# Counting the second sort's blocks on ScalarE, half of them ahead of the first projection loop

## The chip, the cores and the metric

The kernel runs on one core of a Trainium2 chip. The metric is the device time of one execution in microseconds (us). Five engines with their own instruction queues share the work: TensorE (PE in the profile, its weight loads PEld), VectorE (DVE), ScalarE (ACT), GpSimd (POOL), and SyncE (SP), which here only starts transfers. They meet only at semaphores. Before and after were timed in the same manner; three runs of the kernel before are shown here.

## The reference

Two layers of a graph network over 3125 nodes with 256 features and 50,000 edges. Each layer adds a sum over edges, an attention over all nodes, and a mixture of experts. What matters here is the first layer's part over edges and its attention:

```python
xn = _layernorm(x, axis=-1)
x = x + _L0_gnn_ref(xn, edge_index, edge_weight, ...) + _L0_mix_ref(xn[None], ...)[0]

# in _L0_mix_ref
qkv = x @ W_qkv + b_qkv
q, k, v = jnp.split(qkv, 3, axis=2)
q = q - jnp.mean(q, axis=2, keepdims=True)
k = k - jnp.mean(k, axis=2, keepdims=True)
q2 = q * q
k2 = k * k
q2s = jnp.sum(q2, axis=2, keepdims=True)
k2s = jnp.sum(k2, axis=2, keepdims=True)
k2 = _l2_normalize(k2 / (k2s + EPS_DIV), axis=-2)
q2 = _l2_normalize(q2 / (q2s + EPS_DIV), axis=-1)
kv = jnp.einsum('bnc,bnd->bcd', k2, v)
t2 = jnp.einsum('bnc,bcd->bnd', q2, kv) / math.sqrt(N)
attn = v + t2
return attn @ W_out + b_out
```

Layer 0 sums its edges by source node (`segment_sum(vals, src)`), layer 1 by destination node (`segment_sum(msg, dst)`). The kernel therefore sorts the edges twice, once by each.

## The kernel before

The program is a chain of stages with a barrier between them. The change lies in the first, `stage_project0`, which does three things side by side.

**Two counting sorts of the edges.** The 50,000 edges lie as 128 x 391 numbers. The first sort puts them into 25 bins by source, the second into 98 blocks of 32 nodes by destination (100 are counted, 4 in each of 25 turns). A sort has these steps: the bin of each edge (`split_index`); the count of each bin in each partition (`rank_count_bins`: DVE compares all 391 bins with one number and adds up the hits with the same instruction, line 114); sums over partitions by two matmuls on PE (`ps_rank`); the starts of the bins (`rank_bases`); and for each bin the slot of every edge in it (`rank_slots_bins`: compare, running sum, predicated copy, lines 139, 142 and 145). From the slot comes the row to which an edge's record is written.

**The first sort's scatter on POOL.** `scatter_records` issues one indirect DMA for each of the 391 columns (line 245). It waits for `s_rows` twice: at column 0, for the rows of the first 48 columns, which DVE makes first (`SLOT_GROUPS`), and at column 48, for those of the remaining 343. The stage ends when all scatters have landed, and the next stage reads the sorted list.

**The first projection and the attention.** After the sort's rows DVE makes the statistics of x (lines 199 to 214), signals `s_var`, waits until ACT has taken the root (`s_std`), and makes a few products of weights. Then 25 turns over tiles of 125 nodes, spread over three engines:

- PE transposes the normed tile, adds the tile before last to `ps_kv` and `ps_cn` (`add_kv`), and, once ACT has copied the transposed tile to SBUF (`keep_xT`, signal `s_xTs`), multiplies by the weights (line 781).
- DVE adds the biases (from line 675), norms a tile two ahead (line 669), counts four of the second sort's blocks (line 114), turns ACT's sums into negative means (line 687), and scales k2 (lines 690 to 694).
- ACT copies xT of the next tile (line 497), copies q and k with their sums (507), waits for the negative means, squares q and k (510, 511), squares again (514), and waits for k2 and squares it (516). Each accumulating instruction is followed in the profile by a read of the accumulator.

Behind the loop PE closes its sums (lines 805, 806), waits for `s_cnt`, and makes the second sort's sums over partitions (809, 810). A second loop of 25 turns follows, called the slot loop here: PE and ACT make the attention's output, DVE adds it to x (lines 744 to 748) and makes the slots of four blocks (`rank_slots_bins`). `Order` numbers an engine's own steps so that it can wait for its own results: `settle` waits for all of them, `settle_alone` does so with a separate instruction.

Of the kernel before, what the change touches and what calls it, by code (L numbers as in the profile page):

```python
# [12 lines left out]
BF16 = mybir.dt.bfloat16  # L13
# [4 lines left out]
P = 128  # L18
# [3 lines left out]
TN = 25  # L22
# [148 lines left out]
def split_index(o, whole, rest, key, size):  # L171

    o.done(o.eng.tensor_scalar(whole, key, -(size - 1) / 2.0, 1.0 / size, ALU.add, ALU.mult))
    o.settle()
    o.done(o.eng.tensor_scalar(whole, whole, MAGIC, MAGIC, ALU.add, ALU.subtract))
    o.settle()
    o.done(o.eng.scalar_tensor_tensor(rest, whole, -float(size), key, ALU.mult, ALU.add))
    o.settle()
# [110 lines left out]
def stage_project0(nc, a, k):  # L289
# [5 lines left out]
    with ExitStack() as ctx:  # L295
# [30 lines left out]
        first = m.sb("first", [P, P])  # L326
        pad = m.sb("pad", [P, 4 * G0_TILES])
# [61 lines left out]
        s_rows = m.sem("rows_known")  # L389
        s_scat = [m.sem(f"scattered{i}") for i in range(2)]  # L390
# [100 lines left out]
        def _(act):  # L491
            o = Order(act, s_a)
            act.wait_ge(s_var, 1)
# [5 lines left out]
            def step(t, last):  # L499
                if not last:  # L500
                    keep_xT(t + 1)
                o.enter(t, 3) if not last else None
# [13 lines left out]
                nc.scalar.activation(k4[:], k2[:], ACT.Square).then_inc(s_k4, 1)  # L516
                o.leave(TN - 1) if not last else None
# [6 lines left out]
            act.sem_inc(s_sq, 1)  # L524
            act.wait_ge(s_kvd, 1)
# [25 lines left out]
        def _(dve):  # L551
# [62 lines left out]

            for n, g in enumerate(SLOT_GROUPS):
# [9 lines left out]
                nc.vector.tensor_copy(row0[:, g], running[:, 0, g]).then_inc(s_rows, 1)  # L625
            group_bins(o, k["bin0"][:], column, reached, ps_vf, ps_qk, iota_g, G0_BINS, G0_N + 8, s_col, s_row, 0)

            o.done(nc.vector.tensor_copy(key[:], dst[:]))
            o.done(nc.vector.memset(k["record1"][:], 0.0))  # L630
            o.done(nc.vector.memset(cnt[:], 0.0))
            o.settle()
            split_index(o, rest[:], whole[:], key[:], G1_BINS)
            o.done(nc.vector.scalar_tensor_tensor(bin_of1[:], rest[:], -NOWHERE, whole[:], ALU.mult, ALU.max))
            o.done(nc.vector.tensor_scalar(slot[:, ELAST:], k["iota"][:, 0:EC - ELAST], float(P), float(P * G1_N + P - 1), ALU.mult, ALU.add))
            o.done(nc.vector.tensor_copy(k["record1"][:, :, 0], src[:]))
            o.done(nc.vector.tensor_copy(k["record1"][:, :, 1], rest[:]))
# [34 lines left out]
            def step(t, norm_ahead):  # L672
                o.enter(t, 3 + R1) if not isinstance(t, int) else None
# [11 lines left out]
                rank_count_bins(o, bin_of1[:], cnt, mask, k["iota"], t * R1, R1)  # L685
# [19 lines left out]
            o.settle()  # L705
            dve.sem_inc(s_cnt, 1)
# [2218 lines left out]
```

## Time and profile before

| | us |
|---|---|
| three runs: lowest, median, highest | 2844.44, 2845.75, 2851.44 |
| profiled execution, its time | 2843.54 |
| its span, first to last instruction | 2841.8 |
| DVE busy in the span | 1835.1 (65%) |
| POOL busy | 1814.0 (64%) |
| PE busy | 1659.2 (58%) |
| ACT busy | 850.7 (30%) |
| line 245, this stage's scatters | 391 issues, 414.0 busy, 159.7 idle ahead of them |

The engines' shares are means over the whole span. The first stage fills the first 580 us of it, and what counts for it is read there: which engine's last instruction the next stage waits for. The time of the profiled execution is 1.7 us above its span, which is what lies around the first and the last instruction.

### The profile page before, as it was taken

Reading aid. Unit: us, or ns where it says so; the run is one execution under the profiler, and the core shown is the slowest. Engines: PE = TensorE matmul, PEld = TensorE weight load, DVE = VectorE, ACT = ScalarE, POOL = GpSimd, SP = SyncE. Lnnn points to the kernel's source line nnn. Section 1 sums busy time; section 2 is a strip of 40 time slices with the busy share of each in tenths; the row PEclk is TensorE's granted clock in tenths of the full one; section 3 lists DMA queues with packets and bytes.
Section 4 is the critical chain, followed back from the end, with each engine's and each line's share of the span. In section 5 each row is a group of like instructions: output and inputs, shape, how many; then the busy total and the mean of one; then the engine's idle time right before and its main releaser. Section 6 shows DMA issues by size and latency. Waiting matters only on the chain. (4 is left out here: it accounts for less than half of the span.)

```text
span 2841.8 us, 52033 instructions
## 1 busy us (share of the span) xinstructions
PE 1659.2 (58%) x12361; PEld 1202.8 (42%) x12362; DVE 1835.1 (65%) x5560; ACT 850.7 (30%) x2657; POOL 1814.0 (64%) x1828
## 2 busy tenths in 40 slices
PE   0488444236666666424999657655666655401997
PEld 0254333124444454312666434344555544301665
DVE  8776699568777777621222256488888888865322
ACT  0144111024444444101333234323333333301231
POOL 3777777757777777777777777377777777600000
PEclk9999666568888888657999878767666676655998
DMA  7000000053333333042333330233333337321000
GB/s 225 9 22 20 2 2 1 1 197 105 107 107 107 107 106 106 21 168 89 86 87 86 100 90 21 46 106 106 105 106 106 106 106 150 82 69 58 10 18 18
DMA packets 169775, 224.90 MB, mean 79 GB/s; under 512 B 77731, under 2 KB 129226, under 8 KB 169513
## 3 DMA queue, kind: packets, MB, share of 16 engines
q0 software_dynamic: 74368, 138.96, 18.3%
q1 hardware_dynamic: 95270, 84.55, 10.4%
q14 instruction: 105, 0.86, 0.1%
q8 instruction: 32, 0.52, 0.1%
HBM read 184.08 MB, written 39.29 MB: 79 GB/s over the span
## 5 line engine op out<-in xcount | busy, mean ns | idle before, releaser
L2112 POOL DMA_INDIRECT e_rows<-mid_table,rec x488 | 486.1, 996 | 184.1 <-issue 137.7
L245 POOL DMA_INDIRECT mid_sorted<-p_record,p_row x391 | 414.0, 1059 | 159.7 <-issue 122.2
L922 POOL DMA_INDIRECT e_rows<-mid_table,e_rec x440 | 420.0, 954 | 150.4 <-issue 91.4
L245 POOL DMA_INDIRECT mid_sorted<-keep_record,keep_row x391 | 393.7, 1007 | 129.4 <-issue 121.1
L1084 PE MATMUL e_ps_A<-e_rows,e_hot 128*125 128x260 f32 x880 | 306.5, 481 | 0.0
L2374 ACT ACTIVATE room<-room 128x66 f32 x488 | 126.1, 258 | 260.7 <-ACT room L2374 209.8
L1084 PEld LDWEIGHTS e_ps_A<-e_rows,e_hot 128*125 128x125 f32 x880 | 188.0, 237 | 25.1
L1069 PE MATMUL e_ps_T<-e_identb,e_hot 128*125 128x128 bf16 x446 | 84.7, 279 | 185.0 <-DVE e_hot L945 184.0
L1443 DVE COPY x_hidden<-x_ps_h 128x512 f32<-128x512 f32 x64 | 44.3, 692 | 220.3 <-PE x_ps_h L1472 220.3
L2439 PE MATMUL e_ps_mT<-keep_ident,room 128*128 128x128 f32 x488 | 118.2, 423 | 116.4 <-DVE room L2136 116.4
L965 DVE TENSOR_TENSOR e_rows<-e_rows 128x512 f32<-128x512 f32 x220 | 150.8, 685 | 1.8 <-ACT e_rows L1049 1.4
L2439 PEld LDWEIGHTS e_ps_mT<-keep_ident,room 128*128 128x128 f32 x488 | 95.8, 223 | 126.4 <-issue 126.2
L1069 PEld LDWEIGHTS e_ps_T<-e_identb,e_hot 128*125 128x125 bf16 x446 | 50.4, 159 | 206.0 <-DVE e_hot L945 205.2
L1472 PE MATMUL x_ps_h<-w,x_xT 128*128 x256 | 127.8, 622 | 15.4 <-ACT x_xT L1421 15.1
L2163 DVE SCALAR_TENSOR_TENSOR room<-room,e_scale,e_ps_A 128x65 f32<-128x65 f32 x488 | 135.6, 278 | 0.7 <-issue 0.2
L1488 PE MATMUL x_ps_y<-x_w,x_hT 128*128 x512 | 122.4, 382 | 1.6 <-ACT x_hT L1428 1.6
L1041 ACT ACTIVATE acc<-e_state 125x260 f32 x220 | 92.4, 420 | 97.8 <-DVE e_state L973 97.1
L142 DVE TENSOR_TENSOR_SCAN p_running<-p_ones,p_first,p_mask 128x391 f32<-128x391 f32 (+1 forms) x125 | 116.4, 994 | 5.3 <-DVE p_mask L139 5.3
L836 PE MATMUL p_ps_mix<-p_kw,p_qvT 128*125 128x256 f32 x100 | 50.1, 655 | 119.5 <-DVE keep_x L748 118.5
L945 DVE TENSOR_SCALAR e_hot<-keep_iota,e_rec 128x125 f32<-128x125 f32 x446 | 117.0, 375 | 1.1
L1488 PEld LDWEIGHTS x_ps_y<-x_w,x_hT 128*128 128x128 f32 x512 | 95.8, 189 | 44.8 <-issue 30.7
L2811 PE MATMUL f_ps_h<-f_xT,f_w 128*128 (+2 forms) x320 | 99.2, 459 | 20.5 <-DVE f_w L2746 12.4
(526 smaller groups left out, 4023.9 us busy)
## 6 DMA issues: line engine op xcount, KB each, us to landing
mid_expert_in<-p_zrow SPq DMA_DIRECT2D x1, 8192.0 KB
w<-in_L_ffn_w SPq DMA_DIRECT2D x16, 512.0 KB
x_w<-in_L_ffn_w SPq DMA_DIRECT2D x16, 512.0 KB
x_xs<-mid_expert_in SPq DMA_DIRECT2D x64, 128.0 KB
x_b<-in_L_ffn_b SPq DMA_DIRECT2D x64, 128.0 KB
mid_expert_out<-x_y SPq DMA_DIRECT2D x64, 128.0 KB
e_rows<-mid_table,rec POOLq DMA_INDIRECT x488
e_rows<-mid_table,e_rec POOLq DMA_INDIRECT x440, 2.8
```

Of the source, the lines that this page charges most:

```text
L245: pool.indirect_dma_start(out=to, out_offset=bass.IndirectOffsetOnAxis(ap=row[:, t:t + 1].bitcast(U32), axis=0), in_=record[:, t, :], in_o ...
L922: pool.indirect_dma_start(out=rows[:, s % RING * 2 + j, :], out_offset=None, in_=k["table"], in_offset=bass.IndirectOffsetOnAxis(ap=rec[:, ...
L945: last = nc.vector.tensor_scalar(hot[:, q * 2 + j, :], k["iota"][:, 0:NP], rec[:, bass.ds(s * 2 + j, 1), 1:2].rearrange("p a b -> p (a b)" ...
L965: nc.vector.tensor_tensor(r, r, spread(w, P, 2, H, HD), ALU.mult).then_inc(s_wm, 1)
L1069: last = nc.tensor.transpose(ps_T[q % 2][0:NP, j, 0:P], halves[:, :, 1], identb[:])
L1084: last = nc.tensor.matmul(ps_A[0:NP, q % 4, 0:ROW], hot[:, q * 2 + j, :], rows[:, q * 2 + j, :], start=j == 0, stop=j == 1)
L1472: last = nc.tensor.matmul(ps_h[q % 2][:], xT[:, q % 2, c, :], k["w1"][:, bass.ds(e, 1), c, :].rearrange("p a f -> p (a f)"), start=c == 0, ...
L1488: last = nc.tensor.matmul(ps_y[q % 2][:], hT[:, c, :], w2[:, bass.ds(e, 1), c, :].rearrange("p a d -> p (a d)"), start=c == 0, stop=c == F ...
L2112: pool.indirect_dma_start(out=rows[:, j, q, :], out_offset=None, in_=k["table1"], in_offset=bass.IndirectOffsetOnAxis(ap=rec[:, i * TG + q ...
L2163: v.scalar_tensor_tensor(state[:, j, q, 0:W1], before, scale[:, j, q:q + 1], sums_of(j)[:, q // HALF, q % HALF * W1:(q % HALF + 1) * W1], ...
L2374: nc.scalar.activation(acc[:, bass.ds(block_of, 1), :].rearrange("p a w -> p (a w)"), state[:, j, q, :], ACT.Copy).then_inc(s_keep, 1)
L2439: last = nc.tensor.transpose(ps_mT[:, q // HALF, q % HALF * P:(q % HALF + 1) * P], marked[:, q, :], k["ident"][:])
```

## The change

Three new tiles are added (`minus`, `apart`, `equal`) and one semaphore (`s_bins`). ACT gets a function `count_two(b)`, which counts two blocks in four instructions. The square of (bin - b) is 0 where the edge is in block b and at least 1 elsewhere; 1 minus that square, cut off below 0, is 1 or 0; the second instruction adds these up into `cnt`. ACT counts blocks 0 to 49 ahead of the root and the first projection loop, and blocks 50 + 2t and 51 + 2t in turn t. DVE's counting of the second sort goes away, 4 blocks a turn. DVE makes the second sort's bins between the two slot groups of the first sort (`second_bins`), without the memset of `record1`. The signal `s_cnt` to PE, once DVE's, is now ACT's.

```diff
@@ scalar
             o = Order(act, s_a)
+            AHEAD = R1 * TN - 2 * TN
+            def count_two(b):
+                o.settle_alone()
+                for j in range(2):
+                    o.done(nc.scalar.activation(apart[:, j], bin_of1[:], ACT.Square, bias=minus[:, bass.ds(b + j, 1)]))
+                o.settle_alone()
+                for j in range(2):
+                    o.done(nc.scalar.activation(equal[:, j], apart[:, j], ACT.Relu, scale=-1.0, bias=k["one"][:, 0:1],
+                                                accum_out=cnt[:, bass.ds(b + j, 1)]))
+
+            act.wait_ge(s_const, 9)
+            o.done(nc.scalar.activation(minus[:], k["iota"][:], ACT.Copy, scale=-1.0))
+            o.settle()
+            act.wait_ge(s_bins, 1)
+            for b in range(0, AHEAD, 2):
+                count_two(b)
             act.wait_ge(s_var, 1)
             nc.scalar.activation(rstd[:], rstd[:], ACT.Sqrt, bias=k["eps5"][0:NP, :]).then_inc(s_std, 1)
...
                 wait_alone(act, s_k2, t + 1)
                 nc.scalar.activation(k4[:], k2[:], ACT.Square).then_inc(s_k4, 1)
+                count_two(AHEAD + t * 2)
                 o.leave(TN - 1) if not last else None
...
             o.settle()
             act.sem_inc(s_sq, 1)
+            act.sem_inc(s_cnt, 1)
@@ vector
+            def second_bins():
+                o.done(nc.vector.tensor_copy(key[:], dst[:]))
+                o.done(nc.vector.memset(cnt[:], 0.0))
+                o.settle()
+                split_index(o, rest[:], whole[:], key[:], G1_BINS)
+                o.done(nc.vector.scalar_tensor_tensor(bin_of1[:], rest[:], -NOWHERE, whole[:], ALU.mult, ALU.max))
+                o.done(nc.vector.tensor_copy(k["record1"][:, :, 1], rest[:]))
+                o.settle()
+                nc.vector.sem_inc(s_bins, 1)
...
                 nc.vector.tensor_copy(row0[:, g], running[:, 0, g]).then_inc(s_rows, 1)
+                if n == 0:
+                    second_bins()
             group_bins(o, k["bin0"][:], column, reached, ps_vf, ps_qk, iota_g, G0_BINS, G0_N + 8, s_col, s_row, 0)
-            o.done(nc.vector.tensor_copy(key[:], dst[:]))
-            o.done(nc.vector.memset(k["record1"][:], 0.0))
-            o.done(nc.vector.memset(cnt[:], 0.0))
-            o.settle()
-            split_index(o, rest[:], whole[:], key[:], G1_BINS)
-            o.done(nc.vector.scalar_tensor_tensor(bin_of1[:], rest[:], -NOWHERE, whole[:], ALU.mult, ALU.max))
             o.done(nc.vector.tensor_scalar(slot[:, ELAST:], k["iota"][:, 0:EC - ELAST], float(P), float(P * G1_N + P - 1), ALU.mult, ALU.add))
             o.done(nc.vector.tensor_copy(k["record1"][:, :, 0], src[:]))
-            o.done(nc.vector.tensor_copy(k["record1"][:, :, 1], rest[:]))
...
-                rank_count_bins(o, bin_of1[:], cnt, mask, k["iota"], t * R1, R1)
                 wait_alone(dve, s_sum, t * 2 + 2)
...
-            o.settle()
-            dve.sem_inc(s_cnt, 1)
             dve.wait_ge(s_base, 2)
```

The names in the rows of the built program below are those of the tiles with the stage's letter (`p_` for this stage, `keep_` for what later stages keep). First DVE between the two slot groups of the first sort, before:

```order
L625 CAST p_row<-p_running 128x48 [waits p0_vector_steps]
L619 UNCONDITIONAL_BRANCH
L619 ISA
L139 ISA [waits p0_vector_steps]
L139 TENSOR_SCALAR p_mask<-p_bin_of,keep_iota 128x343
```

and after:

```order
L660 CAST p_row<-p_running 128x48 [waits p0_vector_steps]
L641 CAST p_key<-p_dst 128x391
L642 MEMSET p_cnt 128x128
L173 TENSOR_SCALAR p_rest<-p_key 128x391 [waits p0_vector_steps]
L175 TENSOR_SCALAR p_rest<-p_rest 128x391 [waits p0_vector_steps]
L177 SCALAR_TENSOR_TENSOR p_whole<-p_rest,p_key 128x391 [waits p0_vector_steps]
L645 SCALAR_TENSOR_TENSOR p_bin_of<-p_rest,p_whole 128x391 [waits p0_vector_steps]
L646 COPY keep_record<-p_rest 128x391
L654 UNCONDITIONAL_BRANCH [waits p0_vector_steps]
L654 ISA
L139 ISA [waits p0_vector_steps]
```

Seven instructions of the second sort now stand between the rows of the first 48 columns and the loop over the rest.

ACT at its start, before (the first copy of xT follows the root at once):

```order
L490 UNCONDITIONAL_BRANCH [waits barrier_Pool_Activation_PE_DVE_SP_release]
L494 ACT_TABLE_LOAD
L494 ACTIVATE p_rstd<-p_rstd,keep_eps 125x25 [waits p0_variance]
L497 ACTIVATE p_xT<-p_ps_T 128x250 [waits p0_xT_made]
L520 UNCONDITIONAL_BRANCH
L520 ISA
L497 ACTIVATE p_xT<-p_ps_T 128x250 [waits p0_xT_made]
```

and after, first the beginning and then the end of the 25 calls of `count_two`:

```order
L494 UNCONDITIONAL_BRANCH [waits barrier_Pool_Activation_PE_DVE_SP_release]
L511 ACT_TABLE_LOAD
L511 ACTIVATE p_minus<-keep_iota 128x128 [waits p0_const]
L504 ACTIVATE p_apart<-p_bin_of,p_minus 128x391 [waits p0_scalar_steps,p0_second_bins]
L504 ACTIVATE p_apart<-p_bin_of,p_minus 128x391
L507 ACTIVATE p_equal,p_cnt<-p_apart,keep_one 128x391 [waits p0_scalar_steps]
L507 ACTIVATE p_equal,p_cnt<-p_apart,keep_one 128x391
```

```order
L507 ACTIVATE p_equal,p_cnt<-p_apart,keep_one 128x391 [waits p0_scalar_steps]
L507 ACTIVATE p_equal,p_cnt<-p_apart,keep_one 128x391
L517 ACT_TABLE_LOAD
L517 ACTIVATE p_rstd<-p_rstd,keep_eps 125x25 [waits p0_variance]
L520 ACTIVATE p_xT<-p_ps_T 128x250 [waits p0_xT_made]
```

The root and the load of its table stand behind 100 instructions that count, and another table is loaded first.

ACT's turn of the first projection loop, from the squares of q and k on, before:

```order
L510 ISA [waits p0_negative_means,p0_kv_added]
L510 ACTIVATE p_q,p_qsum<-p_qk,p_sums 125x256
L511 ACTIVATE p_k,p_ksum<-p_qk,p_sums 125x256
L101 ISA
L514 REGISTER_ALU [waits p0_scalar_steps]
L514 ACTIVATE p_q,p_q4sum<-p_q 125x256
L516 ACTIVATE p_k<-p_k 125x256 [waits p0_k2_ready]
L520 REGISTER_ALU
L520 COMPARE_AND_BRANCH
```

and after, from the square of k2 on:

```order
L539 ACTIVATE p_k<-p_k 125x256 [waits p0_k2_ready]
L101 REGISTER_ALU
L504 ISA [waits p0_scalar_steps]
L504 ACTIVATE p_apart<-p_bin_of,p_minus 128x391
L504 ISA
L504 ACTIVATE p_apart<-p_bin_of,p_minus 128x391
L101 REGISTER_ALU
L507 REGISTER_ALU [waits p0_scalar_steps]
L507 ACTIVATE p_equal,p_cnt<-p_apart,keep_one 128x391
L507 REGISTER_ALU
L507 ACTIVATE p_equal,p_cnt<-p_apart,keep_one 128x391
L544 REGISTER_ALU
```

Four instructions that count and a wait between them stand between the square of k2 and the next turn's copy of xT, which stands at the turn's head.

## Rows read from the trace of the kernel before

**Rows 1.** The timeline at the stage's end: start us, us, engine, line, op

```profile
576.44 0.96 POOL L245 DMA_INDIRECT mid_sorted<-p_record,p_row  x1 [0.30 <-issue]
...
586.02 0.55 DVE L978 CAST e_rec<-e_rec 128x440 int32<-128x440 f32 x1 [41.86 <-DMA e_abb<-in_L_gnn_ab]
```

**Rows 2.** Busy by stretch, scatters of line 245: length, POOL busy (count), clock

```profile
118.00:280.00 162.00, 122.07 (x127) 0.98 0.10 22
308.00:544.00 236.00, 185.59 (x159) 0.64 0.02 1
545.00:578.00 33.00, 24.78 (x26) 0.50 0.03 2
```

**Rows 3.** The timeline of DVE before the first loop

```profile
39.54 0.19 DVE L625 CAST p_row<-p_running 128x48 int32<-128x48 f32 x1
...
87.23 0.37 DVE L625 CAST p_row<-p_running 128x343 int32<-128x343 f32 x1
...
89.59 0.34 DVE L629 CAST p_key<-p_dst 128x391 f32<-128x391 int32 x1
90.04 0.71 DVE L630 MEMSET keep_record<- 128x782 f32 x1
...
93.44 0.74 DVE L199 BATCH_NORM_STATS2 p_st<-keep_x  x2
```

**Rows 4.** Line 245 alone, 40 to 106.5 us: min/median/max, first and last start

```profile
L245 POOL DMA_INDIRECT mid_sorted<-p_record,p_row x48: 954/987/1348, 40.6 to 105.4; - x48
```

**Rows 5.** Groups of instructions by line and shape, ACT: busy, mean ns | idle

```profile
L541 ACT ACTIVATE p_qvT<-p_ps_T 128x500 f32<-128x500 f32 x25 | 14.7, 587 | 190.3 <-PE p_ps_T L830 190.3
...
L511 ACT ACTIVATE p_k<-p_qk,p_sums 125x256 f32<-125x256 f32 x25 | 12.3, 492 | 0.0
...
L514 ACT ACTIVATE p_q<-p_q 125x256 f32 x24 | 10.0, 417 | 4.3 <-ACT p_k L511 4.3
```

**Rows 6.** The timeline of ACT and DVE, one turn of the first loop

```profile
123.38 0.38 ACT L497 ACTIVATE p_xT<-p_ps_T 128x250 f32<-128x250 f32 x1
...
123.92 0.42 ACT L507 ACTIVATE p_qkc<-p_qk 125x256 f32<-125x256 f32 x1 [0.15 <-DVE p_qk L675]
...
124.64 0.19 ACT L507 ACTIVATION_READ_ACCUMULATOR p_qkc<-p_qk 125x1 f32 x1
...
127.02 0.17 DVE L687 TENSOR_SCALAR p_sums<-p_sums 125x2 f32<-125x2 f32 x1
...
127.43 0.51 ACT L510 ACTIVATE p_q<-p_qk,p_sums 125x256 f32 x1 [2.60 <-DVE p_sums L687]
...
129.51 0.42 ACT L516 ACTIVATE p_k<-p_k 125x256 f32<-125x256 f32 x1 [0.29 <-DVE p_k L694]
...
129.89 0.38 ACT L497 ACTIVATE p_xT<-p_ps_T 128x250 f32<-128x250 f32 x1
```

**Rows 7.** Line 114 alone, DVE's counting: min/median/max

```profile
L114 DVE TENSOR_SCALAR_CACHE_REDUCE p_mask<-p_bin_of,keep_iota x125: 603/618/623, 11.1 to 277.0; 128x391 bf16<-128x391 bf16 x125
```

**Rows 8.** Line 494 alone, in the timeline and as a line

```profile
102.90 0.32 ACT L494 ACTIVATE p_rstd<-p_rstd,keep_eps 125x25 f32<-125x25 f32 x1 [100.83 <-DVEq L641]
...
L494 ACT ACT_TABLE_LOAD  x1: 1283/1283/1283, 0.8 to 0.8; - x1
```

**Rows 9.** Line 675 alone, first instruction of DVE's turn: first and last start

```profile
L675 DVE TENSOR_TENSOR p_qk<-p_ps_qk,p_bias x25: 684/691/693, 116.6 to 274.0; 125x512 f32<-125x512 f32 x25
```

**Rows 10.** The timeline of PE, products of one turn

```profile
125.01 1.96 PE L781 MATMUL p_ps_qk<-p_w,p_xT 128*125 128x512 f32 x4
...
128.52 0.50 PE L781 MATMUL p_ps_a<-p_wa,p_xT 128*125 128x8 f32 x4
```

**Rows 11.** Line 744 alone, first instruction of the slot loop's turn

```profile
L744 DVE TENSOR_TENSOR p_part<-p_ps_mix,p_bout x25: 424/425/426, 307.1 to 532.4; 125x256 f32<-125x256 f32 x25
```

**Rows 12.** The timeline of PE, the same four matmuls before and after idling

```profile
268.52 1.12 PE L787 MATMUL p_ps_kv<-p_v,p_k 125*128 x4 [0.87 <-ACT p_k L516]
...
280.69 2.05 PE L787 MATMUL p_ps_kv<-p_v,p_k 125*128 125x256 f32 x4 [4.87 <-ACT p_k L516]
```

More of the change, by code:

```diff
@@ L326, in stage_project0 @@
         first = m.sb("first", [P, P])
+        minus = m.sb("minus", [P, P])
+        apart = m.sb("apart", [P, 2, EC], BF16)
+        equal = m.sb("equal", [P, 2, EC], BF16)
         pad = m.sb("pad", [P, 4 * G0_TILES])
@@ L389, in stage_project0 @@
         s_rows = m.sem("rows_known")
+        s_bins = m.sem("second_bins")
         s_scat = [m.sem(f"scattered{i}") for i in range(2)]
@@ L492, in _ @@
             o = Order(act, s_a)
+            AHEAD = R1 * TN - 2 * TN
+            assert AHEAD % 2 == 0 and AHEAD + 2 * TN <= P
+            def count_two(b):
[12 more added lines that the diff above has]
+                count_two(b)
             act.wait_ge(s_var, 1)
@@ L501, in step @@
                     keep_xT(t + 1)
-                o.enter(t, 3) if not last else None
+                o.enter(t, 3 + 4) if not last else None
                 q2t = q2[:, bass.ds(t, 1), :].rearrange("p a d -> p (a d)")
@@ L672, in step @@
             def step(t, norm_ahead):
-                o.enter(t, 3 + R1) if not isinstance(t, int) else None
+                o.enter(t, 3) if not isinstance(t, int) else None
                 wait_alone(dve, s_proj, t + 1)
```

## The prediction

> **What bounds the kernel now.** I read first which engine the first stage ends on, then whether that engine can be reached by the change at all, and last how much room the other engines have. The stage's end is in the timeline [rows 1]: POOL's last scatter starts at 576.44 and ends at 577.4 us, and when the next stage's records arrive at 586.02, DVE has been idle for 41.86 us, so its last instruction had ended at 544.2. So the stage ends on POOL, with DVE 33.2 us early. POOL issues 391 scatters one behind the other. In stretches of its own line [rows 2] there are 26 in 33 us at the end, where DVE is silent: one every 1.26 us, of which it is busy for 24.78/26 = 0.95. In the first projection loop (118 to 280) it is one in 162/127 = 1.28 us, in the slot loop (308 to 544) one in 236/159 = 1.48 us. Nothing but "issue" lies between them: POOL waits for DVE only at scatter 0 (rows of the first 48 columns, ready at 39.7 [rows 3]) and at scatter 48 (rows of the rest). The bound of the stage is thus DVE's chain up to 39.7 us and then POOL's own 391 issues. The change touches neither. What is left to work out is whether it pushes DVE's end past 577.4.
>
> **Second bins earlier on DVE.** Before, DVE made the second sort's bins between 89.59 and 93.44 us, 3.85 us with a memset of 0.71 us [rows 3]. After, they stand between the two slot groups. That leaves out the memset and the 0.4 us that stay behind, so they take about 2.9 us; the bins are ready at 39.7 + 2.9 + 0.1 = 42.7 and everything of the second slot group moves by 2.9 us. Who waits for it: POOL at scatter 48. It needs those rows when its 48 first scatters are out, the last of which starts at 105.4 [rows 4], so at about 106.7; they were ready at 87.6 [rows 3] and will be at 90.5. Cover: 16 us, cost nothing. DVE has the 2.9 us back after the group, and the memset's 0.7 on top: the statistics of x are finished near 102.3 instead of 102.8.
>
> **The first 50 blocks on ACT.** One count_two is 2 squares, a wait, 2 rectified lines with an accumulator read each, a wait. ACT does not show a 391-element instruction. From above and below: 500 elements take 587 ns [rows 5] and 250 take 380 ns [rows 6], so an element is 0.83 ns; the 256-element square with a bias from SBUF takes 492 ns [rows 5], and 135 elements more make it 604 ns. In the timeline [rows 6] an activation starts about 0.09 us before the one ahead has ended, and a read of the accumulator adds 0.10 us to the pitch (123.92 to 124.64 for two, less one activation). So: squares 0.51 + 0.60 = 1.11; wait 0.18 (ACT's wait for itself in this loop, the gap ahead of the second square of q, 4.3 us over 24); two lines at a pitch of 0.61, the last with its read 0.70, 1.31; wait 0.18. That is 2.79 us for two blocks, 1.39 a block, against DVE's 0.54 (its instructions of 618 ns [rows 7] follow each other every 0.54). 25 of them: 69.7 us, from 42.9 to 112.6. As outer bounds: no dearer than the 587 ns of 500 elements plus the 0.10 us of the bias and a read, four times (some 3.1 us), no cheaper than four times 0.42 plus the waits (2.0).
>
> There stands a new wait behind them: the square root that gives DVE its standard deviations is queued on ACT after all 25. Before, ACT did it at 102.90, at once, since it had idled for 100.83 us [rows 8]. The table with the root, loaded before in that idle time, is now loaded again directly ahead of it, 1.28 us [rows 8]. So the root ends near 112.6 + 1.3 + 0.3 = 114.2 instead of 103.2, and DVE's whole chain behind it (weights' products, first norm, the loop) moves by **11 us**.
>
> **Two blocks per turn.** DVE loses 4 x 0.54 = 2.16 us of a turn. Its turns start from 116.6 to 274.0 in 24 steps [rows 9]: 6.56 us each. ACT idles 2.60 us ahead of the square of q, waiting for DVE's sums [rows 6], which stood behind the counts. ACT's turn afterwards, from the start of one copy of xT to the next: copy and both sums of q and k 123.38 to 124.83, less the 0.15 that it waited, 1.30; round trip to DVE's sums with DVE now free, 0.55 (0.2 to reach it, 0.17, 0.24 back, from 127.02 and 127.43); square of q to end of k4, 127.43 to 129.93, 2.50; counts 2.79 less the last wait, 2.61, less 0.09 overlap; loop 0.05. Sum **6.9 us** (6.1 and 7.2 with the outer bounds). PE cannot hide it: the products 125.01 to 129.02 (4.0 us, [rows 10]) need the copy of xT, which now stands behind count_two. But copy plus products plus transposes are some 5.2 us and PE's adding of kv fits beside, so ACT's 6.9 is the longest ring. The loop does not get faster, it gets 0.34 x 24 = **8.2 us** longer, with ACT its bound instead of DVE. The last turn's counts end some 3.2 us after k4 starts, and PE comes to the sums over partitions about 5 us after that (its closing products lie between), so they cost nothing.
>
> **The sum.** DVE's slot loop begins at 307.1 and its turns start until 532.4 [rows 11], every 9.39 us, and do not depend on the change. DVE ends at 544.2 + 11 + 8.2 = 563.4, say 563. POOL still ends at 577.4. 14 us of cover are left of 33.2. All 25 turns of the slot loop, which are what slows POOL, still lie inside its scatters, so what they cost it (159 x (1.48 - 1.26) = 35 us) stays. Change of the time: 0. The profiled execution took 2843.5 us with a span of 2841.8; the three timed ones have the median 2845.75, and that is the forecast.
>
> **Rules of the skill.** The count loop's row says that POOL's scatters lose next to nothing to the counting form on DVE: mean 122.07/127 = 0.96 us in it, 0.95 in the silent end [rows 2]. The Trainium skill, "SBUF — State Buffer", section "Who interferes with whom", lets copies, casts and tensor_scalar on VectorE lock GpSimd out of a shared port pair, but exempts the form that writes its accumulator; by the lock taken broadly the change would free POOL, by the exemption it does not, and the trace agrees with the exemption. Speaking against the change is a rule of "ScalarE: Activation LUTs", section "Rules for kernel authors", of the Trainium skill: simple arithmetic such as relu belongs on VectorE, up to three times faster there. The rows give 1.39 against 0.54 us a block, so this holds here, and more so since one instruction becomes two.
>
> **The rivals.**
> (a) *ACT's turn eats the cover, slower.* DVE ends after POOL if the loop's turn exceeds 6.56 + (33.2 - 11)/24 = 7.5 us. Against: my sum is 6.9, from rows of the same loop. For: the accumulated line reads and writes places that change by turn, register work sits ahead of each instruction, and PE waits longer in each turn. After 4.87 us of idle PE took 2.05 us for four matmuls that otherwise take 1.12 [rows 12]: at that rate the products alone last twice as long. With a turn of 8.5 us DVE ends at 544.2 + 11 + 24 x 1.94 = 601.8, 24 past POOL: 2870. With the outer bound of count_two everywhere (3.1 us a call, 7.2 a turn) DVE ends at 544.2 + 19 + 15 = 578, level with POOL. At the low clock throughout (11 us a turn) it would be some 85 to 90 us: near 2935.
> (b) *ACT is quicker than I think.* With a turn of 6 us DVE ends at 542. The time is the same, 2845.8, since POOL ends it.
> (c) *POOL gains from a lighter DVE.* At most the 127 scatters go from 1.28 to 1.26 us: 1.8 us, 2844. For it speaks only that small difference.
> (d) *The pace of the later stages.* POOL's schedule and all that starts on it stand as they were; a shift of PE's idle time before 586 us could change its clock in the next stages either way. I see no row that prices it.
>
> **How the numbers follow.** Forecast 0.74, (b) 0.10, (c) 0.04, (a) 0.08, (d) towards faster 0.04. What a measurement of this kernel can tell from no change is about 0.3%, 8.5 us. Forecast, (b) and (c) lie inside: 0.88. Slower 0.08, faster 0.04. The range holds the first three: the median of 3 within the spread of the runs of before (2844.4 to 2851.4), less 1.8 for (c) and a few us for the clock of PE later, plus the near end of (a), a turn of 7.8 us, 7 us: 2840 to 2855.
>
> **What would show it.** Right: POOL's scatters of the first list from 40.6 to about 577 with no wait at scatter 48; ACT's root near 114; DVE's turns every 6.9 us from about 127.7 on, with PE waiting for ACT's copy of xT; DVE's slot loop from about 326 to 563; next stage at 586. Wrong: DVE's last instruction after 577, a turn above 7.5, or PE's clock well under 0.98 in the loop; POOL's pitch outside the slot loop under 1.26.

## The result, and the profile after

The changed kernel takes 2861.41 us (median of six runs, 2857.66 to 2865.4), the kernel before 2844.85 in the same measurement. The ratio is 1.0056, 95% interval 1.0043 to 1.0069: some 16 us slower. That is under 1%, but clear of the noise. The forecast was no change, with a range that ended at 2855. The profiled execution of the changed kernel took 2865.4 us, with a span of 2863.7.

First the stage that the prediction worked on. The timeline of the changed kernel around its end, the counterpart of [rows 1]; columns are start us, us, engine, line, operation:

```profile
552.37 0.36 DVE L780 CAST keep_row<-p_running 128x391 int32<-128x391 f32 x1
...
579.99 0.95 POOL L245 DMA_INDIRECT mid_sorted<-p_record,p_row  x1 [0.30 <-issue]
589.63 0.55 DVE L1005 CAST e_rec<-e_rec 128x440 int32<-128x440 f32 x1 [36.90 <-DMA e_abb<-in_L_gnn_ab]
```

DVE ends at 552.7 and POOL at 580.9, 28 us later. The cover of 33 us has shrunk and not gone; the next stage starts 3.6 us later than in [rows 1]. The timeline of ACT and DVE before the loop, the counterpart of [rows 8]:

```profile
42.61 1.13 ACT L504 ACTIVATE p_apart<-p_bin_of,p_minus 128x391 bf16<-128x391 bf16 x2 [38.87 <-DVEq L648]
43.84 0.62 ACT L507 ACTIVATE p_equal<-p_apart,keep_one 128x391 bf16<-128x391 bf16 x1
...
45.24 1.13 ACT L504 ACTIVATE p_apart<-p_bin_of,p_minus 128x391 bf16<-128x391 bf16 x2
...
108.99 1.28 ACT L517 ACT_TABLE_LOAD   x1
110.28 0.32 ACT L517 ACTIVATE p_rstd<-p_rstd,keep_eps 125x25 f32<-125x25 f32 x1
...
110.63 0.32 DVE L673 RECIPROCAL p_rstd<-p_rstd 125x25 f32<-125x25 f32 x1 [8.22 <-ACT p_rstd L517]
```

And the first instruction of DVE's turn in the first loop, the counterpart of [rows 9], and one instruction of its turn in the slot loop (two lines behind that of [rows 11]), with first and last start:

```profile
L705 DVE TENSOR_TENSOR p_qk<-p_ps_qk,p_bias x25: 691/692/693, 125.5 to 286.6; 125x512 f32<-125x512 f32 x25
its engine sat idle before it (us, times) until:
  PE p_ps_a L808: 31.0, 25
...
L771 DVE TENSOR_TENSOR p_part<-p_ps_mix,p_bout x25: 409/412/425, 318.4 to 540.9; 125x256 f32<-125x256 f32 x25
```

The order of things is as the prediction has it: the table load ahead of the root, DVE waiting for it, then a loop in which DVE waits for PE and PE for ACT's copy (29.1 us in 23 of the turns). The turn is 161.1/24 = 6.71 us.

The loss is elsewhere. Comparing the starts of the big groups in the two traces, the changed kernel is 4.3 us late at the end of the first layer's edges and 5.7 at the start of the second layer's; in that stage, which the change doesn't touch, it loses 16.5 more. The stage's gathers are indirect DMAs by which POOL fetches rows for the edges, eight for each turn of DVE. By line, before and after (instruction durations min/median/max in ns, first and last start in us):

```profile
L2112 POOL DMA_INDIRECT e_rows<-mid_table,rec x488: 942/946/1852, 1837.2 to 2470.7; - x163
```

```profile
L2139 POOL DMA_INDIRECT e_rows<-mid_table,rec x488: 942/946/2132, 1842.9 to 2492.9; - x163
```

The groups by line show where in it (busy us, mean ns, then POOL's idle time ahead of them):

```profile
L2112 POOL DMA_INDIRECT e_rows<-mid_table,rec x488 | 486.1, 996 | 184.1 <-issue 137.7 <-POOLq L266 35.7 <-PE e_ps_A L2447 10.7
```

```profile
L2139 POOL DMA_INDIRECT e_rows<-mid_table,rec x488 | 502.6, 1030 | 183.0 <-issue 137.4 <-POOLq L266 34.7 <-PE e_ps_A L2474 11.0
```

POOL waits no longer than before; the gathers themselves take 16.5 us more, all in the long ones, for the median is the same. POOL issues them one behind the other, so that it bounds the stage. What changed beside them is DVE's first instruction of a turn, the product of line 2163 (2136 before):

```profile
L2136 DVE TENSOR_TENSOR room<-e_hot,e_rows x61: 1219/1226/1236, 1852.4 to 2473.4; 128x1024 f32<-128x1024 bf16 x61
its engine sat idle before it (us, times) until:
  DMA e_rows<-mid_table,rec: 50.1, 55
```

```profile
L2163 DVE TENSOR_TENSOR room<-e_hot,e_rows x61: 1217/1225/1286, 1857.5 to 2495.6; 128x1024 f32<-128x1024 bf16 x61
its engine sat idle before it (us, times) until:
  DMA e_rows<-mid_table,rec: 32.6, 27
  issue: 31.7, 10
```

Ten idles of 3.0 to 3.45 us with nothing to wait for, where there was none. The loop of this stage has eleven passes of four turns, so ten branches back (a pass is one run through the loop's body), and the ten idles stand one each behind a branch, at the head of the body, 43 us apart. What follows one of them, on POOL and DVE in the changed kernel:

```profile
1993.55 1.23 DVE L2163 TENSOR_TENSOR room<-e_hot,e_rows 128x1024 f32<-128x1024 bf16 x1 [3.17 <-issue]
1994.10 1.50 POOL L2139 DMA_INDIRECT e_rows<-mid_table,rec  x1 [0.30 <-issue]
...
2003.29 1.22 DVE L2163 TENSOR_TENSOR room<-e_hot,e_rows 128x1024 f32<-128x1024 bf16 x1
2003.64 1.68 POOL L2139 DMA_INDIRECT e_rows<-mid_table,rec  x1 [0.30 <-issue]
...
2013.15 1.22 DVE L2163 TENSOR_TENSOR room<-e_hot,e_rows 128x1024 f32<-128x1024 bf16 x1
2013.19 2.00 POOL L2139 DMA_INDIRECT e_rows<-mid_table,rec  x1 [0.30 <-issue]
...
2023.47 1.23 DVE L2163 TENSOR_TENSOR room<-e_hot,e_rows 128x1024 f32<-128x1024 bf16 x1 [0.68 <-DMA e_rows<-mid_table,rec]
2024.32 1.20 POOL L2139 DMA_INDIRECT e_rows<-mid_table,rec  x1 [0.30 <-issue]
```

Each of the four gathers issued while the product runs ends 2.03 to 2.05 us after the product's start, whenever it began: 1994.10 + 1.50, 2003.64 + 1.68, 2013.19 + 2.00, 2024.32 + 1.20. A gather that starts 0.04 us behind the product takes 2.00 us, one that starts 0.85 us behind it 1.20, and one alone 0.95. It is so in the whole trace: 56 gathers that were issued during this product and took longer than 0.96 us end 0.81 to 0.82 us after its end. What counts is which of the two comes first, for of the 49 gathers that were already running when a product started, 46 took 0.94 to 0.95 us. In the kernel before DVE is ahead, waits for each gather's rows, and so its product starts some 0.85 us before a gather, turn for turn (the 44 gathers issued during a product in the loop's eleven passes take 1.21 us on average):

```profile
1994.11 1.23 DVE L2136 TENSOR_TENSOR room<-e_hot,e_rows 128x1024 f32<-128x1024 bf16 x1 [0.65 <-DMA e_rows<-mid_table,rec]
1994.96 1.19 POOL L2112 DMA_INDIRECT e_rows<-mid_table,rec  x1 [0.30 <-issue]
```

After an idle DVE is late, starts its products as soon as it can, and they land on the gathers until it has caught up, three turns later. In the pass shown that is (1.50 + 1.68 + 2.00) - 3 x 1.20 = 1.6 us. The passes differ, though, and a second product of two SBUF tiles takes part, that of `e_hot` and `e_ex`, 2.4 us or more behind the first. Added up gather by gather over both traces, the gathers issued during the first product take 13.9 us more than before, those during the second 3.3 us more, and all others 0.7 us less: the 16.5 us. The Trainium skill, "SBUF — State Buffer", section "Who interferes with whom", says that a VectorE instruction with two SBUF inputs contends with a GpSimd instruction that reads SBUF; the product has two, and the trace agrees.

Why does DVE idle? All of an engine's instructions lie one behind the other in its program, and a loop's body is a piece of it. The changed kernel's DVE program is 21 instructions shorter ahead of this loop, whose body has 292: it starts at instruction 1347 instead of 1368 of the built program. **Theory P**: the place of the body in the program decides whether its head is still held when the branch goes back to it. The Trainium skill, "Runtime: NRT & Kernel Launch", section "Instruction fetch mechanics", says that a taken branch to outside the two pages held forces a fetch before execution goes on. **Rival T**: the later start, another lead of POOL over DVE, or something else that the change does to the data or the pace.

The profile has a row that tells of fetches, the packets of the DMA queue that brings instructions (packets, MB, share). For the whole span, in the changed kernel and in the changed kernel with 21 fillers (below):

```profile
q14 instruction: 105, 0.86, 0.1%
```

```profile
q14 instruction: 56, 0.46, 0.1%
```

Most of the difference falls in the loop in question. In the 400 us from 1950 to 2350 there are these:

| kernel | packets | idles at the loop's head |
|---|---|---|
| changed | 50 | DVE |
| changed, 21 fillers | 3 | none |
| before | 49 | ACT |
| before, 20 fillers on ACT | 3 | none |
| before, 218 fillers on DVE | 97 | DVE (ACT's fetches are there, its idles hidden) |
| before, 228 on DVE, 20 on ACT | 50 | DVE |

Each engine whose loop stalls brings some five packets a pass; where neither stalls there are 3 packets in all. In the pass shown five of them lie between 1986 and 2000 us, around the idle that ends at 1993.55. So the idle is a fetch of instructions, as theory P has it; how the held part is laid out is not shown.

### The profile page after: what moved, and what is told of

The parts are those of the page before. It is cut to its first block and busy times, and to the rows that moved or that the text cites. A ratio compares the mean times of both kernels' runs of the same rounds, so it can differ in the third digit from the quotient of the medians.

```text
span 2863.7 us, 52240 instructions
## 1 busy us (share of the span) xinstructions
PE 1667.6 (58%) x12361; PEld 1208.4 (42%) x12362; DVE 1779.1 (62%) x5359; ACT 966.8 (34%) x2959; POOL 1836.4 (64%) x1828
## 5 line engine op out<-in xcount | busy, mean ns | idle before, releaser
L2139 POOL DMA_INDIRECT e_rows<-mid_table,rec x488 | 502.6, 1030 | 183.0 <-issue 137.4
L1111 PE MATMUL e_ps_A<-e_rows,e_hot 128*125 128x260 f32 x880 | 314.3, 491 | 0.0
L2163 DVE TENSOR_TENSOR room<-e_hot,e_rows 128x1024 f32<-128x1024 bf16 x61 | 74.6, 1224 | 64.4 <-DMA e_rows<-mid_table,rec 32.6
```

The lines of the kernel that those rows point to most:

```text
L1111: last = nc.tensor.matmul(ps_A[0:NP, q % 4, 0:ROW], hot[:, q * 2 + j, :], rows[:, q * 2 + j, :], start=j == 0, stop=j == 1)
L2139: pool.indirect_dma_start(out=rows[:, j, q, :], out_offset=None, in_=k["table1"], in_offset=bass.IndirectOffsetOnAxis(ap=rec[:, i * TG + q ...
```

## The experiments

Fillers are instructions that do nothing useful in an engine's idle time at the end of its first-stage program, and move what follows:

```diff
+            for i in range(N):
+                nc.vector.memset(filler[0:1, i:i + 1], 0.0)
```

**The changed kernel with 21 of them.** 

> The changed kernel with 21 one-element memsets at the very end of DVE's program of the first stage. There DVE is idle until POOL ends (552.7 against 580.9), so the 21 themselves (about 1.3 us) are hidden. They put every later DVE instruction back to the number in the program that it had before the change: the loop over the edges of the second layer (4 turns a body, 292 instructions on DVE) starts at instruction 1368 again instead of 1347. Theory P (place of the loop in DVE's program): the ten idles of 3.0 to 3.45 us that DVE has once a loop in the changed kernel vanish, that stage takes some 634 us again instead of 650, L2139's long gathers go back from 503 to about 487 us in sum, and the kernel takes 2861.4 - 16 = about 2846 to 2849. Rival T (the later start of the stage or another lead between DVE and POOL makes the stalls): nothing about these has changed, so the ten idles stay and it takes 2861 (2858 to 2865). The Trainium skill, "Runtime: NRT & Kernel Launch", section "Instruction fetch mechanics", says that a taken branch whose target is outside the two pages held forces a fetch before execution goes on, which is theory P's mechanism.

Measured 2849.72 us against 2849.52 of the kernel before, ratio 0.9998 (0.998 to 1.0015). None of the ten idles is there, although the stage starts at the same time as in the changed kernel (first gather at 1843.5, there at 1842.9). The gathers run from 1843.5 to 2475.8 (632.3 us, before 633.5) and are busy for 484.8. The whole loss is gone with all of the change still in. The first stage's scatters end at 578.45. T falls, for this run changes nothing that T speaks of.

**The place alone, in the kernel before.** 

> The kernel before, counting still on DVE, with 235 one-element memsets at the end of DVE's first-stage program (some 14 us, from 544 to about 558, under POOL's 577). DVE's edge loop then starts at instruction 1603, which is 256 after the 1347 of the changed kernel. Theory P with a period of 256 instructions (the Trainium skill, "Runtime: NRT & Kernel Launch", section "Instruction fetch mechanics", gives blocks of 256): ten DVE idles of 3 to 3.5 us appear, one a loop, the edge stage grows from 634 to about 650 us and the kernel from 2845 to about 2858 to 2861, with none of the change in it. Rival T, or a period other than 256: no such idles, 2845 (2842 to 2848).

> The kernel before with 43 one-element memsets in the same place: DVE's edge loop starts at 1411, which is 64 after 1347 but not 256. Theory P with blocks of 256: a shift by 43 leaves the loop where it touches two blocks, no idles, 2845 (2842 to 2848). If the period is 64 instructions instead, the ten idles are there and it takes 2858 to 2861. Rival T: 2845.

The first missed, the second came as expected: 2850.15 (1.0002, 0.9989 to 1.0015) and 2849.36 (0.9994, 0.9981 to 1.0006), no idles in either. So the period is not 256 of the instructions that I count. I then looked for the zone with 192, 204, 216 and 228, in one run each. They also have fillers on ACT, whose idles can't be told from its other waits in these runs; the packets of instructions can.

With 228 and 256: 

> The kernel before with 228 one-element memsets at the end of DVE's first-stage program and 256 one-element copies at the end of ACT's. One of four runs that look for the place that stalls on DVE: if the period is 256 the pads 228, 216, 204 and 192 lie 28, 40, 52 and 64 places ahead of the loop of before, and with a body of 292 the stalling zone is about 36 wide, so one to three of the four show DVE's idles of 3 us and the others none. On ACT 256 is one full period: the idles of 1.5 us of the kernel before are there if the period is 256, and gone otherwise.

With 216 and 250: 

> As the run with 228 and 256, with 216 memsets on DVE and 250 copies on ACT. Period 256: DVE 40 places ahead of before, the likeliest to lie in the zone; idles of 3 us once a loop and some 15 us on the edge stage (2860 to 2865 in all). ACT 6 places ahead of before: the zone is some 15 wide there, idles of 1.5 us about as likely as not. If no place between 192 and 228 stalls, the theory of the loop's place is wrong for DVE and only the time or data theory is left.

With 204 and 262: 

> As above with 204 on DVE and 262 on ACT. DVE 52 places ahead of before, ACT 6 behind it. With the idles on DVE the edge stage takes about 650 us, without them about 634.

With 192 and 270: 

> As above with 192 on DVE and 270 on ACT. DVE 64 places ahead of before, ACT 14 behind it: by a zone of 15 at most one of ACT's pads 250, 262, 270 beside 256 can lie more than 15 from another that stalls. 270 should be free of ACT's idles, as 20 was.

Idles of 2.7 to 3.7 us, ten in each, showed with 204, 216 and 228, none with 192. DVE's body stalls where it starts at 1347, 1572, 1584 and 1596, not at 1368, 1411, 1560 and 1603. The packets tell of ACT too: between 3010 and 3580 us there are 103 or 104 with ACT's pads of 256, 250 and 262, so that both engines fetch, and 4 with 270, where neither does. ACT's body stalls where it starts at 829, 1079, 1085 and 1091, not at 849, 1001 and 1099.

**One filler in the changed kernel.** 

> The changed kernel with one one-element memset at the end of DVE's first-stage program. 21 cured it; a pad of 235 on the kernel before puts the loop 256 instructions behind where the changed kernel has it and did not stall. If a block of code holds one instruction of its own, that pad was one place beyond the changed kernel's, and the stalling zone ends right there: then one memset is enough, no idles, as the kernel before. If the edge lies elsewhere between 1 and 20: the ten idles stay and it takes 16 us more than before. I hold the two about equally likely.

A miss for the guess in it: the ten idles are there (2.7 to 3.1 us), so 1348 stalls too. If the place counts with a period, 1348 stalling and 1603 free put it under 255 instructions of my count, not at the 256 of the expectations. Whether the program as fetched has instructions that the built one doesn't show, or the period is another, stays open.

**A condition in which the times can't tell.** In three sets of runs the kernel before took 4082 to 4090 us and the others 4084 to 4096 (medians), but for one of which the test of ACT's turn below speaks. My expectations lay it to a chip with a lower TensorE clock. That was wrong: two of the three chips ran the kernel before at 2847 and 2853 us at other hours. In the traces signals between engines come late in the first stage while POOL issues DMAs. In the kernel before with 216 fillers ACT's square of q is behind DVE's means by 18.3 us, where [rows 6] show 0.24:

```profile
215.79 0.17 DVE L688 TENSOR_SCALAR p_sums<-p_sums 125x2 f32<-125x2 f32 x1
...
234.24 0.51 ACT L511 ACTIVATE p_q<-p_qk,p_sums 125x256 f32 x1 [19.92 <-remote]
```

TensorE's granted clock is low as well, 0.52 to 0.57 between 200 and 600 us of that trace, near the lower of its two levels; PE is busy there for 12 to 22 us of each 100. What makes the signals late stays open. There POOL waits 209 us for PE in the edge stage, so its gathers don't bound it. The runs that were meant to settle the price and fell in this condition:

> The kernel before with 216 one-element memsets behind DVE's first-stage program, in its idle time, and nothing of the change. Traces with pads of 228, 216 and 204 showed DVE's idle of about 3 us at the head of each edge loop, those with 235, 192 and 43 did not; that one was on a chip on which every kernel took some 4090 us, so its times tell nothing. Theory P (the place of the loop alone costs the time): the idles are back and the edge stage grows by some 16 us, to 2863 where the kernel before takes 2847 (2860 to 2866, ratio 1.005 to 1.007). If the idles are there but cost nothing, some other part of the change cost the 16 us: 2847.

> The kernel before with 217 one-element memsets behind DVE's first-stage program, in its idle time, and nothing of the change. With 216 the trace showed DVE's ten idles of 2.8 to 3.4 us at the head of the edge loop, but on a chip where TensorE is slower, every kernel takes some 4085 us and PE bounds that stage. Where the kernel before takes 2847 us, theory P (the place alone costs the time) expects the edge stage to grow by some 16 us, 2863 (2860 to 2866, ratio 1.005 to 1.007). If the time needs something else of the change: 2847.

> The changed kernel as it is, beside the other two on the same chip. Theory P: the same as the kernel before with 217 memsets, within 4 us, and 16 us (12 to 19) over the kernel before. Where TensorE's clock is low and PE bounds the edge stage: within 5 us of the kernel before, although DVE's ten idles are there.

The changed kernel as it is comes out at 1.0012 (1.0003 to 1.0022) in this condition, the kernel before with 216 fillers at 1.0012 and with 217 at 1.0002 (0.9993 to 1.0012), the one with one filler at 1.0003: stalls that cost some 5 us at most. These runs show the idles, not their price.

**The place alone, where the kernel before takes 2847 us.** 

> The kernel before with 218 one-element memsets behind DVE's first-stage program, in its idle time. Pads of 216 and 217 showed the ten idles at the head of DVE's edge loop, in traces with a lower TensorE clock where PE bounds that stage. Where the kernel before takes 2847 us, theory P (the place of the loop alone costs the time) expects 2863 (2860 to 2866), the edge stage some 16 us longer. If the time needs something else of the change: 2847. Where it takes some 4085 us: within 5 us of it.

Measured 2853.94 against 2846.66: 1.0021 (1.0009 to 1.0033), 7 us. The ten idles are there (2.9 to 3.4 us), the gathers last 642.3 us instead of 633.5. So the place alone costs time, but half of what I expected, and 9 us of the change were left. Two things differed from the changed kernel: the place within the zone, and ACT's loop of the same stage, of which a test below speaks (with 218 fillers ACT's fetches are there too, 97 packets for both engines, but beside a late DVE it shows no idles over 1.2 us). The last run had both near the changed kernel's:

> The kernel before with 228 one-element memsets behind DVE's first-stage program and 20 one-element copies behind ACT's, nothing of the change. DVE's edge loop starts at 1596, ten places nearer to the border behind which the stalls end than with 218; ACT's at 849, where it showed no idles. If the 9 us that the pads of 218 did not show are a matter of the exact places, 2860 to 2866, the edge stage 648 to 652 us, gathers of 1.7 to 2.1 us in the turns behind the stalls. If they come from something else of the change: 2854, as with 218. Where every kernel takes some 4085 us it tells nothing.

Measured 2869.73 against 2853.36: 1.0056 (1.0039 to 1.0073), the same ratio as the change. The time lies above the 2860 to 2866 of the expectation, in a set in which the kernel before is 7 us above that of the last one; the edge stage, expected at 648 to 652 us, is above it too. The idles are 3.1 to 3.45 us, the gathers last 655.0 us, those of the changed kernel 650.0:

```profile
L2118 POOL DMA_INDIRECT e_rows<-mid_table,rec x488: 942/949/2090, 1843.5 to 2498.5; - x163
...
L2142 DVE TENSOR_TENSOR room<-e_hot,e_rows x61: 1212/1224/1299, 1858.1 to 2501.3; 128x1024 f32<-128x1024 bf16 x61
its engine sat idle before it (us, times) until:
  issue: 32.8, 10
```

The whole slowdown is thus had with nothing of the change in the kernel. Which of the two differences made 7 into 16 us was not separated. The idles' length is alike, and what differs is when the products fall. Gather by gather, the first product costs 7.9 us more than in the kernel before with 218 fillers and 14.4 with 228, the second product nothing and 7.0. For example, with 218 fillers the pass at 2033 has gathers of 1.33, 1.50 and 2.00 us, with 228 the pass at 2038 has 1.60, 1.69, 1.91 and 1.50.

**ACT's place.** 20 one-element copies at the end of ACT's first-stage program in the kernel before. 

> The kernel before with 20 one-element copies at the end of ACT's first-stage program, in its idle time. ACT's body of the same loop (271 instructions) then starts at instruction 849 instead of 829. In the kernel before ACT has nine idles of 1.4 to 1.7 us, once a loop; in the changed kernel, where it starts at 1001, none. Theory P: one block border fewer inside the body, the nine idles vanish; ACT is not the bound of the stage, so the time moves by 0 to -5 us (2840 to 2846). Rival T: the nine idles stay and 2845.

Measured 2848.62 (0.9997, 0.9983 to 1.001); the nine idles of ACT of 1.4 to 1.7 us, once a pass (a tenth, of 0.96 us, is in the trace as well), are gone, and so are the packets of instructions, 3 where the kernel before has 49. The same effect on a second engine, and no gain, since DVE and POOL don't wait for ACT there. It is hidden, DVE's isn't.

**Lateness without a stall.** Is it the fetch that slows POOL, or that DVE is late? The traces already speak against the fetch: all 30 gathers that overlap the ten idles of the changed kernel take 0.94 or 0.95 us, and the kernel before with 49 packets in its loop has gathers of 486.1 us, that with 20 fillers on ACT and 3 packets 487.1. In the kernel before, at the head of each pass of DVE's loop:

```diff
+                for _ in range(3):
+                    o.done(v.memset(late[:], 0.0))
+                    o.settle()
```

> The kernel before with three memsets of 1180 elements at the head of each body of DVE's edge loop, some 3.2 us, and no stall for code. Where the kernel before takes 2847 us: theory L (a late DVE puts its products on top of POOL's gathers) some 15 us more (2858 to 2867), with gathers of 1.7 to 2.0 us behind the memsets; rival F (the fetch of code slows the gathers) 2847 to 2850. Where it takes some 4085 us neither shows: 4 to 8 us more, as measured.

Measured 2860.42 against 2846.66: 1.004 (1.0024 to 1.0056), 14 us. The gathers last 651.3 us and are busy for 503.9. The timeline behind one set of memsets:

```profile
1990.61 1.04 DVE L2326 MEMSET e_late<- 128x1180 f32 x1 [0.31 <-DVE e_late L2326]
...
1991.89 1.23 DVE L2137 TENSOR_TENSOR room<-e_hot,e_rows 128x1024 f32<-128x1024 bf16 x1 [0.24 <-DVE e_late L2326]
1992.67 1.27 POOL L2113 DMA_INDIRECT e_rows<-mid_table,rec  x1 [0.30 <-issue]
...
2011.21 1.22 DVE L2137 TENSOR_TENSOR room<-e_hot,e_rows 128x1024 f32<-128x1024 bf16 x1
2011.40 1.85 POOL L2113 DMA_INDIRECT e_rows<-mid_table,rec  x1 [0.30 <-issue]
```

The same picture with no fetch on DVE: there are 49 packets, as in the kernel before. The memsets of 1990.61 and before don't lengthen the gathers beside them; the products do, in the turns after. The fetch as such costs POOL nothing that shows. The lateness is not quite the same as in the changed kernel: with the gaps between them the memsets put the product back by 4.4 us, not 3.2, and there are eleven sets of them for ten idles. So the run shows that lateness alone costs such a time, and not that the same lateness costs the same. Two earlier runs of this kernel fell in the 4085 us condition and gave 1.0019 (1.0009 to 1.0028) and 1.0018 (1.0008 to 1.0028):

> The kernel before with three memsets of 1230 elements (about 1.04 us each by the 0.84 us a 1000 of the wide memset at 588.5) at the head of each body of DVE's edge loop, so that DVE comes some 3.3 us late once a loop without any stall for code; they write a buffer of their own that nothing reads. In the changed kernel DVE makes the 3.2 us good within three turns, POOL never waits, and yet its gathers take 16 us more, since the products of a late DVE start together with a gather (up to 2.0 us instead of 0.95) rather than 0.8 us ahead of it (1.2). Theory L (lateness alone does it): the edge stage again grows by 12 to 20 us, 2861 (2858 to 2867), with gathers of 1.7 to 2.0 us in the turns behind the memsets. Rival F (the fetch of code itself slows POOL's gathers): at most 3 us more, 2847 to 2850.

> The kernel before with three memsets of 1200 elements at the head of each body of DVE's edge loop, some 3.3 us, no stall for code. Theory L (a late DVE puts its products on top of POOL's gathers): some 15 us more (2858 to 2867), gathers of 1.7 to 2.0 us behind the memsets. Rival F (the fetch of code itself slows the gathers): 2847 to 2850. Where PE bounds the stage neither shows.

**The rival of ACT's turn.** The changed kernel with 21 fillers and all four blocks of a turn counted on ACT in the loop:

```diff
-            for b in range(0, AHEAD, 2):
-                count_two(b)
...
-                count_two(AHEAD + t * 2)
+                count_two(t * 4)
+                count_two(t * 4 + 2)
```

> The changed kernel (with the 21 memsets that cure the edge loop) without the first half of the counting ahead of the loop: ACT counts four blocks in each turn. It tests the rival in which ACT's turn eats DVE's cover. A turn was 6.71 us with two blocks and count_two 2.63, so 9.3 us; the root is back at 103.2. DVE ends at 544.2 + 24 x (9.3 - 6.56) = 610, 32 us past POOL's 577.5: 2847 + 30 = about 2877 (2870 to 2885), with PE waiting longer for ACT's copy of xT. If the loop hid the counts better than that (a turn under 7.9) it would cost nothing.

It ran only in the 4085 us condition: 4131.54 against 4083.49, 1.0113 (1.0096 to 1.013). The next stage's records come at 1021.95 instead of 978.08 of the changed kernel in that condition. So ACT can lengthen the stage, but in this condition POOL ends its scatters at 565 us and the stage ends on DVE in any case. The 2877 us of the expectation were not tested.

## Why the prediction was wrong

- *What bounds the first stage*: right. POOL ends it, with 28 us of cover left (14 were forecast; 25 of them against the 577.4 of the forecast), and a kernel with the whole change and the loop put back takes the time of the kernel before.
- *Second bins*: the 2.9 us were right; ACT starts at 42.6, forecast 42.7 to 42.9.
- *The first 50 blocks*: count_two is (45.24 - 42.61) = 2.63 us, forecast 2.79 (its terms add up to 2.78): the square took 607 ns (604 forecast) and the line 614, but the waits between them cost less than 0.18. The root starts at 110.28 and DVE goes on at 110.63 instead of 103.25: 7.4 us, forecast 11.
- *Two blocks per turn*: 6.71 us a turn, forecast 6.9; its ring is the forecast one. The round trip of 0.55 in it is 0.61 by its own three terms, which would have made the forecast worse. The loop is 3.7 us longer, forecast 8.2. Both terms, the 11 and the 8.2 us, were sized too large and lie under POOL's cover, so they cost nothing. The slot loop, said not to depend on the change, is 2.8 us shorter (318.4 to 540.9 against [rows 11]); no run looks for the reason.
- *POOL's end* at 580.9 against 577.4 in the two profiled executions: kernels with the same first stage end it between 575.6 and 583 in the other traces, so I read nothing from it.
- *The rivals*: (a) didn't come, a turn stayed under 7.5; (b) came in part, with the turn between 6 and 6.9 us; (c) didn't, the scatters beside the loop have 120.44/126 = 0.96 us as in [rows 2]; and (d) is where it failed.
- **The step that failed** is the sentence "POOL's schedule and all that starts on it stand as they were", and with it the sum, which ended at the first stage. (d) said that the later stages' pace could change, priced it at nothing, leaned on PE's clock, and gave it 0.04 towards faster. The right mechanism was not among the rivals: the change makes DVE's program 21 instructions shorter and ACT's 172 longer, and everything behind moves. DVE's edge loop of the second layer, started 21 instructions earlier in the program, fetches at its head in each pass, comes 3.0 to 3.45 us late and so lengthens POOL's gathers by 16.5 us. The numbers for it stood in the built program, and the trace of before had the symptom on ACT: an idle with no releaser, once a pass, in a loop of 271 instructions. Its price stood there too, in gathers of 1.2 us beside a product against 0.95.

## What to carry to other kernels

A change that adds or removes instructions moves every later loop of that engine. For loop bodies as long as the two here (292 instructions on DVE, 271 on ACT; shorter ones were not tried) look where they start before and after, and in the trace for an idle with no releaser at the head once a pass. The row of instruction packets on the profile's page tells it even where the idle is hidden behind another wait. Such a stall may be cured with a few instructions in idle time ahead (21 did here, 1 did not), and has nothing to do with what the change does. And where POOL issues back to back, an engine with slack is still not free: DVE late by 3 us, made good three turns on, cost 1.6 us in a pass because its two-input products no longer kept their phase to POOL's DMAs. None of the kernels here beats the one before.

## What was not expected of the hardware

- A gather issued while DVE's 1.23 us product of two SBUF tiles runs ends 0.81 to 0.82 us after the product's end, and so takes up to 2.00 us; alone it takes 0.95 us, and also when it is already running as the product starts.
- A loop head that has to be fetched makes DVE idle for 2.6 to 3.7 us a pass and ACT for 1.0 to 2.1, and brings some five packets of the instruction queue a pass.
- The same kernels on the same chips took 2847 us at one hour and 4085 at another, with signals of 0.24 us taking 18. In that condition PE is waited for in the edge stage, and the idles of DVE cost some 5 us or less.
